# Latents' attention: four operations of the middle tiles move from VectorE to GpSimd

## The chip, the cores and the metric

The kernel runs on one core of one Trainium2 chip. The metric is the device time of one execution in microseconds (us). The engines are named as in the profile: PE (TensorE), DVE (VectorE), ACT (ScalarE), POOL (GpSimd), SP (SyncE, which only issues DMAs). Each works through its own list in the order of the program; they meet through semaphores only.

## The reference, cut to what matters

Sixteen samples of 64 latents go through a cross-attention on 1601 image tokens each, then a differential self-attention, then a mixture of 8 experts. The change lies in the self-attention.

```python
x = x + xattn(ctx_1024, layernorm(x))          # over 90% of the time
x = x + attn(layernorm(x))                     # the part that is changed
x = x + ffn(layernorm(x))                      # gates and 8 experts

# attn: 16 heads, two sub-heads of 8 each
Q, K, V = proj(Wq), proj(Wk), proj(Wv);  Q1, Q2 = split(Q);  K1, K2 = split(K)
attn = softmax(causal(Q1 K1^T / sqrt(8))) - lam * softmax(causal(Q2 K2^T / sqrt(8)))
O = attn @ V                                   # 16 heads x 16
O = O / sqrt(mean(O * O) + EPS) * rms_scale * (1 - 0.8)
return concat_heads(O) @ Wo.T
```

The 1024 latents are handled as 8 tiles of 128 rows (`TB = 8`).

## The kernel before, in words

The cross-attention fills the first 860 us. The self-attention of the 8 tiles and the experts come after it, in functions whose names begin with `tail_`: `tail_vector` is what DVE does, `tail_gpsimd` POOL, `tail_scalar` ACT, `tail_tensor` PE. Each loops over `m` from 0 to 7, and the loops are skewed against each other so that several tiles are under way. The order on each engine is written out by hand, and nothing reorders it.

What one tile t goes through, with the names used below:

- PE projects its queries and keys into PSUM (`project`), ACT copies the queries (`queries`, tile `Qs`), DVE multiplies the keys by a 0/1 mask into four spread copies (`keys`, tile `Kx`, 128x1024), and PE forms the scores in two halves (`self_scores`).
- DVE takes the maximum of each row and subtracts it, per half (`maxima`, tiles `amx` and `region`), ACT takes the exponential (`exp`), PE transposes (`transpose_exponentials`), ACT copies (`weights`), PE multiplies with the values (`weigh_values`; its semaphore is `pv`).
- DVE's `combine` divides by the sums (`arc`, `t12`), adds the two sub-heads (`Ob`), squares (`Osq`), sums (`oms`, semaphore `ms`) and scales the sum (semaphore `ms2`). POOL raises it to the power -0.5 (`inverse_rms`, semaphore `ms3`). DVE's `group_norm` multiplies (`Oc`).
- PE transposes `Oc` (`side_transposes`), ACT copies it (`side_copies`), PE multiplies by Wo (`side_products`, semaphore `side1`), DVE adds the result to x and takes the layer norm's statistics (`side_reads`, semaphore `var`), POOL takes the power for it (`ln_deviation`, semaphore `rstd`), DVE normalises (`ln_normalise`, semaphore `h2`), and PE transposes that for the experts.

Iteration m of DVE's loop is: `combine(m-1)`, `side_reads(m-1)` (which works on tile m-2), first half of `maxima(m+1)`, `keys(m+2)`, `group_norm(m-1)`, `ln_normalise(m-2)`, second half of `maxima(m+1)`. For m = 7 there are no maxima or keys, and the first part of the gates (`first0`) stands in their place. POOL's loop runs over n: `inverse_rms(n)`, then `ln_deviation(n-1)`; DVE's iteration m goes with POOL's n = m-1. For n = 3 there are two `ln_deviation`, and for n = 1 `outputs_low` follows, which belongs to the last sample of the cross-attention.

PE's iteration m is: `side_transposes(m-1)`, first half of `self_scores(m+1)`, `side_products(m-1)`, `project(m+2)`, `project_values(m+1)`, `transpose_exponentials(m, 0..1)`, second half of `self_scores(m+1)`, `transpose_exponentials(m, 2..3)`, `weigh_values(m)`. On ACT `side_copies(m-1)` stands right behind `exp` of the second half of tile m. So a side product needs the second half's maxima of the iteration before.

Of the kernel before, what the change touches and what calls it, by code (L numbers as in the profile page):

```python
# [18 lines left out]
ALU = mybir.AluOpType  # L19
# [22 lines left out]
TB = 8  # L42
SH, SD = 16, 8
# [113 lines left out]
def perceiver(nc, x, ctx_in, ln1_g, ln1_b, ln2_g, ln2_b, Wq, Wkv, Wo, aWq, aWk, aWv, aWo,  # L157
              lq1, lk1, lq2, lk2, rms_scale, gate_w, gate_b, expert_w, expert_b, out):
    es = ExitStack()
    with es:  # L160
        def sb(name, shape, dt=F32):
            return es.enter_context(nc.sbuf_tensor(name, shape, dt))
# [93 lines left out]
        pick = sb("pick", [128, 4])  # L256
# [291 lines left out]

        Qs = [sb(f"Qs{p}", [128, 2, 128]) for p in range(2)]
        Kx = [sb(f"Kx{p}", [128, 2, 4, 128]) for p in range(2)]
        VW = SD * 2 + 1
        Vb = [sb(f"Vb{p}", [128, 2, SH, 2, VW]) for p in range(2)]
# [41 lines left out]
        def side(n):  # L596
            return Turn(n - 1)
# [163 lines left out]
        def wait(eng, name, turn):  # L761
            eng.wait_ge(ta[name].sem, ta[name].upto(turn))

        def first(turn):
            return turn.off == 0
# [4 lines left out]
        def bc(ap, n):  # L770

            return ap.unsqueeze(len(ap.shape)).to_broadcast(list(ap.shape) + [n])
# [13 lines left out]
        def keys(dve, t, src):  # L786
# [4 lines left out]
            p_ = pick[:].unsqueeze(1).to_broadcast([128, 2, 4]).unsqueeze(3).to_broadcast([128, 2, 4, 128])  # L791
            nc.vector.tensor_tensor(Kx[t.off % 2][:], k_, p_, ALU.mult).then_inc(ta["kx"].sem, 1)

        def tail_vector(dve, link):
            def maxima(t, k):
                dve.wait_ge(ta["scores"].sem, ta["scores"].upto(t, k))
# [9 lines left out]
            def combine(t):  # L806
                wait(dve, "pv", t)
                pv = WW[:, :, 0:16 * VW].rearrange("p c (k d) -> p c k d", d=VW)
                nc.vector.reciprocal(arc[:], pv[:, :, :, 2 * SD]).then_inc(ta["r"].sem, 1)
                wait(dve, "r", t)  # L810
                second = arc[:].rearrange("p c (n a) -> p c n a", a=2)[:, :, :, 1]
                nc.vector.tensor_tensor(second, second, nlam[:].rearrange("p (c n) -> p c n", c=2), ALU.mult)\
                  .then_inc(ta["r2"].sem, 1)
                wait(dve, "r2", t)
                nc.vector.tensor_tensor(t12[:], pv[:, :, :, 0:2 * SD], bc(arc[:], 2 * SD), ALU.mult)\
                  .then_inc(ta["t12"].sem, 1)
                wait(dve, "t12", t)
                if not first(t):
                    wait(dve, "oc", t.plus(-1))
                v = t12[:].rearrange("p c (n a) d -> p (c n) a d", a=2)  # L820
                nc.vector.tensor_tensor(Ob[:].rearrange("p (h d) -> p h d", h=SH), v[:, :, 0, :], v[:, :, 1, :],
                                        ALU.add).then_inc(ta["ob"].sem, 1)
                wait(dve, "ob", t)
                nc.vector.tensor_tensor(Osq[:], Ob[:], Ob[:], ALU.mult).then_inc(ta["sq"].sem, 1)
                wait(dve, "sq", t)
                nc.vector.tensor_reduce(oms[:, 0, :], Osq[:].rearrange("p (h d) -> p h d", h=SH), AX.X, ALU.add)\
                  .then_inc(ta["ms"].sem, 1)
                wait(dve, "ms", t)
                nc.vector.tensor_scalar(oms[:, 1, :], oms[:, 0, :], 1.0 / (2 * SD), EPS, ALU.mult, ALU.add)\
                  .then_inc(ta["ms2"].sem, 1)  # L830

            def group_norm(t):
                wait(dve, "ms3", t)
                if not first(t):
                    wait(dve, "side0", side(t.off))
                nc.vector.tensor_tensor(Oc[:].rearrange("p (h d) -> p h d", h=SH),
                                        Ob[:].rearrange("p (h d) -> p h d", h=SH), bc(oms[:, 2, :], 2 * SD),
                                        ALU.mult).then_inc(ta["oc"].sem, 1)

            def side_reads(n):  # L840

# [67 lines left out]
            for m in range(TB):  # L909
                t = Turn(m)  # L910
                if m > 0:
                    combine(t.plus(-1))
                if m > 1:
                    side_reads(m - 1)
                if m + 1 < TB:
                    maxima(t.plus(1), 0)
                if m + 2 < TB:
                    keys(dve, t.plus(2), W[0][:, 256:512])
                if m == TB - 1:
                    first0, second0 = gating(0)  # L920
                    first0()
                if m > 0:
                    group_norm(t.plus(-1))
                if m > 1:
                    ln_normalise(dve, m - 2).then_inc(ta["h2"].sem, 1)
                if m - 1 == X1_SIDE:
                    ln_normalise(dve, TB).then_inc(ta["h"].sem, 1)
                if m + 1 < TB:
                    maxima(t.plus(1), 1)
                if m == 0:  # L930
                    reciprocals(dve, LAST)
# [24 lines left out]

        def tail_gpsimd(pool):
            def inverse_rms(t):
                wait(pool, "ms2", t)
                nc.gpsimd.tensor_tensor(oms[:, 2, :], oms[:, 1, :], mhalf[:], ALU.pow).then_inc(ta["ms3"].sem, 1)  # L960

            denominators(pool, nc.gpsimd, LAST)
            normalise_outputs(pool, nc.gpsimd, LAST)
            for n in range(TB):
                inverse_rms(Turn(n))
                if n > 0:
                    ln_deviation(pool, n - 1)
                if n == X1_SIDE:
                    ln_deviation(pool, TB)
                if n == 1:  # L970
                    outputs_low(pool, nc.gpsimd, LAST)
            ln_deviation(pool, TB - 1)
            n = 0
            for t in range(0, TB, 2):
                pool.wait_ge(ex_scaled.sem, t // 2 + 1)
                pr = prod[t // 2 % 2]
                for m in (4, 2, 1):
                    n += 1
                    nc.gpsimd.tensor_tensor(pr[:, 0:m, :], pr[:, 0:m, :], pr[:, m:2 * m, :], ALU.add)\
                      .then_inc(tail_pool.sem, 1)  # L980
                    pool.wait_ge(tail_pool.sem, n)
                pool.wait_ge(ex_xb.sem, t // 2 + 1)
                nc.gpsimd.tensor_tensor(xb[:, t, :], xb[:, t, :], pr[:, 0, :], ALU.add).then_inc(ex_even.sem, 1)


        def queries(act, t, src):
            wait(act, "projqk", t)
            nc.scalar.copy(Qs[t.off % 2][:].rearrange("p c n -> p (c n)"), src).then_inc(ta["q"].sem, 1)

        def values(act, t, src):  # L990
            wait(act, "projv", t)
# [10 lines left out]
        def tail_scalar(act, outputs, outputs_high, projected):  # L1002
# [50 lines left out]
            for m in range(TB):  # L1053
                t = Turn(m)
                if m > 1:
                    side_copies(m - 1)
                if m - 1 == PJ_SIDE:
                    projected(LAST)
                if m + 2 < TB:
                    queries(act, t.plus(2), W[0][:, 0:256])  # L1060
                if 0 < m < TB - 1:
                    values(act, t.plus(1), W[1])
                weights(t, 0)
                weights(t, 1)
                if m + 1 < TB:
                    exp(t.plus(1), 0)
                weights(t, 2)
                weights(t, 3)
                if m + 1 < TB:
                    exp(t.plus(1), 1)  # L1070
                if m == 1:
                    for k in range(2):
                        outputs_high(LAST, k)
# [39 lines left out]
        def tail_tensor(pe, side_item, weigh):  # L1113
# [31 lines left out]
            def weigh_values(t):  # L1145
                wait(pe, "vb", t)
                if more(t):
                    wait(pe, "vb", t.plus(1))
                if t.off + 2 < TB:
                    wait(pe, "kx", t.plus(2))  # L1150
                for r in range(4):
                    pe.wait_ge(ta["et_out"].sem, ta["et_out"].upto(t, r))
                    for h in range(4):
                        c, n = h // 2, 2 * r + h % 2
                        for j in range(2):
                            ins = mm(W[c][64 * j:64 * j + 64, 2 * VW * n:2 * VW * n + 2 * VW],
                                     ET[t.off % 2][:, r, h, 64 * j:64 * j + 64],
                                     Vb[t.off % 2][:, j, 8 * c + n].rearrange("p a d -> p (a d)"),
                                     start=True, stop=True)
                ins.then_inc(ta["pv"].sem, 1)  # L1160
# [588 lines left out]
        def _(act):  # L1749
# [125 lines left out]
            def slot(b, prep=True, post=True, stats=True):  # L1875
                old = b.plus(-1)
                for u in range(UNITS):
# [12 lines left out]
                    if b is LAST and u == H_AT:  # L1890
                        early_columns_out(act)
                    if b is LAST and u == TILE0_AT:
                        queries(act, Turn(0), W[0][:, 0:256])
                        values(act, Turn(0), W[1])
                    if b is LAST and u == KEYS1_AT:
                        queries(act, Turn(1), W[0][:, 0:256])
                    if b is LAST and u == VALUES1_AT:
                        values(act, Turn(1), W[1])

# [372 lines left out]
```

## Time and profile before

| | us |
|---|---|
| median of 3 runs (977.25 to 979.66) | 978.41 |
| the profiled execution | 982.4 |
| its span | 980.6 |
| DVE busy in 907.50 to 918.00 (one tile, m = 5) | 10.12 of 10.50 |
| POOL busy in the same stretch | 3.42 of 10.50 |

The profile is that of one execution, and its span starts with the first instruction. PE, PEld (weight loads), DVE, ACT and POOL have their own rows; a row's start plus its duration is its end, and the next instruction of an engine can start a little before that. "idle before" names what ended the engine's wait. PEclk 1.00 is TensorE at 2.4 GHz, 0.50 at 1.2 GHz. In this span DVE's loop iterations m = 2 to 7 begin, with the reciprocal of L809, at 869.50, 883.21, 896.22, 907.58, 917.88 and 927.03, and the last `combine` at 935.30.

### The profile page before, as it was taken

The page shows a single profiled execution, that of the slowest core. Times are in us where ns is not written, and L with a number is a line of the kernel's source. Part 1 is how long each engine was busy: PE and PEld are TensorE (multiplying, and loading weights), DVE is VectorE, ACT ScalarE, POOL GpSimd, SP SyncE. Part 2 cuts the span into 40 slices and gives each one's busy share as a digit, 9 for nine tenths or more (in the row PEclk, how much of TensorE's full clock was granted, in tenths as well). Part 3 has the DMA queues.
Part 4 walks back from the last instruction along what each step waited for, and adds up shares of the span by engine and source line. Part 5 has one row for each costly group of instructions (what it writes and reads, how often), then busy time and mean ns, then how long its engine had stood idle before and what let it go on. Part 6 is the DMA issues. An engine that isn't in the chain of part 4 may idle for free.

```text
span 980.6 us, 20490 instructions
## 1 busy us (share of the span) xinstructions
PE 925.7 (94%) x8246; PEld 497.7 (51%) x8246; DVE 795.9 (81%) x1591; ACT 701.2 (72%) x1003; POOL 377.5 (38%) x376
## 2 busy tenths in 40 slices
PE   8679999999999999999999999999999998979985
PEld 5444445454545454545454545454545454557642
DVE  5969798989798989898979797979897845768945
ACT  4576778786878787878787787878787667545531
POOL 6562134433443435343434333434342304163342
PEclk9799999999999999999999999999999999979977
DMA  6212030302120303030212121121212000000000
GB/s 207 70 21 61 6 86 11 82 12 81 12 80 13 81 12 81 12 81 18 74 22 72 30 63 37 56 35 59 42 39 37 22 2 22 23 3 23 2 6 16
DMA packets 74565, 41.95 MB, mean 43 GB/s; under 512 B 62276, under 2 KB 69864, under 8 KB 74472
## 3 DMA queue, kind: packets, MB, share of 16 engines
q1 hardware_dynamic: 74184, 39.60, 16.2%
q8 instruction: 65, 1.06, 0.4%
q10 hardware_dynamic: 288, 1.05, 0.3%
q14 instruction: 28, 0.23, 0.1%
HBM read 25.98 MB, written 0.59 MB: 27 GB/s over the span
## 4 chain that ended last, share of the span: by engine, by line
PE 79%; DVE 12%; ACT 4%; issue 2%; POOL 1%; DMA 1%; POOLq 0%; ACTq 0%; DVEq 0%
PE S L2122 9%; PE S L2113 9%; PE OA L2146 9%; PE S L2116 8%; PE OA L2152 8%; PE OA L2149 8%; PE WW L2058 8%; PE WW L2085 1%; PE WW L2086 1%; PE WW L2087 1%; PE WW L2045 1%; PE S L1205 1%; DVE region L1517 1%; PE WW L2047 1%; PE WW L2046 1%
## 5 line engine op out<-in xcount | busy, mean ns | idle before, releaser
L1833 ACT ACTIVATE region<-S,sigma 128x1024 f16<-128x1024 f32 x208 | 231.6, 1113 | 142.2 <-PE S L2122 142.2
L1517 DVE TENSOR_TENSOR region<-S,region 128x1024 f16<-128x1024 f32 x208 | 252.4, 1214 | 47.7 <-ACT S L1837 47.6
L1505 DVE TENSOR_REDUCE mx<-WW 128x1 f32<-128x512 f32 (+1 forms) x480 | 262.6, 583 | 29.6 <-PE WW L2058 22.4
L1837 ACT ACTIVATE S<-S,sigma 128x1024 f32<-128x1024 f32 x208 | 224.3, 1078 | 0.0
L1652 POOL TENSOR_TENSOR xk<-raw,xk 128x508 f16<-128x508 f32 x64 | 63.3, 998 | 170.6 <-DVE xk L1384 170.6
L2058 PE MATMUL WW<-xT,region 128*128 128x512 f16 x360 | 124.8, 381 | 4.1 <-DVE region L1496 2.1
L2113 PE MATMUL S<-region,xT 128*128 128x512 f16 (+1 forms) x416 | 124.7, 381 | 3.4 <-DVE region L1517 1.7
L2122 PE MATMUL S<-region,xT 128*128 128x512 f16 (+1 forms) x416 | 124.2, 380 | 0.0
L2116 PE MATMUL S<-region,xT 128*128 128x512 f16 (+1 forms) x416 | 124.2, 380 | 0.0
L2146 PE MATMUL OA<-region,xk 128*128 128x512 f16 (+1 forms) x416 | 123.9, 379 | 0.0
L2149 PE MATMUL OA<-region,xk 128*128 128x512 f16 (+1 forms) x416 | 123.7, 379 | 0.0
L2152 PE MATMUL OA<-region,xk 128*128 128x512 f16 (+1 forms) x416 | 123.7, 379 | 0.0
L538 POOL TENSOR_TENSOR region<-region,rb 128x512 f32<-128x512 f32 x32 | 40.6, 1270 | 128.8 <-DMA rb<-inv_dram 128.8
L546 POOL TENSOR_TENSOR ew<-region,o_hi 128x1024 f16<-128x1024 f32 x32 | 68.0, 2126 | 57.1 <-ACT o_hi L1814 57.1
L1771 ACT ACTIVATE raw<-raw,smc 128x128 f32<-128x128 f32 (+1 forms) x187 | 86.1, 486 | 0.0
L2122 PEld LDWEIGHTS S<-region,xT 128*128 128x128 f16 (+1 forms) x416 | 41.2, 99 | 48.9 <-issue 0.5
L2116 PEld LDWEIGHTS S<-region,xT 128*128 128x128 f16 (+1 forms) x416 | 41.1, 99 | 49.0 <-issue 0.5
L2149 PEld LDWEIGHTS OA<-region,xk 128*128 128x128 f16 (+1 forms) x416 | 40.6, 98 | 49.1
L2152 PEld LDWEIGHTS OA<-region,xk 128*128 128x128 f16 (+1 forms) x416 | 40.6, 98 | 49.1
L2058 PEld LDWEIGHTS WW<-xT,region 128*128 128x128 f16 x360 | 34.9, 97 | 55.7 <-DVE region L1496 14.0
L1641 POOL TENSOR_TENSOR smc<-smc,mhalf 128x13 f32<-128x13 f32 x16 | 38.9, 2433 | 60.5 <-DVE smc L456 60.5
L2113 PEld LDWEIGHTS S<-region,xT 128*128 128x128 f16 (+1 forms) x416 | 34.2, 99 | 44.0 <-issue 17.4
(315 smaller groups left out, 1851.0 us busy)
## 6 DMA issues: line engine op xcount, KB each, us to landing
raw<-ctx SPq DMA_DIRECT2D x16, 768.0 KB
rb<-inv_dram SPq DMA_DIRECT2D x16, 512.0 KB, 3.5
xT<-xk SPq DMA_TRANSPOSE x48, 3.2
left_row<-left_pT SPq DMA_DIRECT2D x48, 2.0 KB
raw<-ctx SPq DMA_DIRECT2D x16, 32.5 KB
WO_lo<-L_xattn_Wq ACTq DMA_DIRECT2D x1, 512.0 KB, 3.8
WO_hi<-L_xattn_Wkv ACTq DMA_DIRECT2D x1, 512.0 KB, 4.7
lx<-x SPq DMA_DIRECT2D x1, 512.0 KB, 6.3
```

The lines of the kernel that those rows point to most:

```text
L1505: nc.vector.tensor_reduce(mx[:, r, c:c + 1], W[BANK[("m", n)]][:, 0:width], AX.X, ALU.max)\
L1517: nc.vector.tensor_tensor(p_lo[k], src, p_hi[k], ALU.subtract).then_inc(lo_done.sem, 1)
L1771: ins = nc.scalar.activation(x_[0:r, t, :], x_[0:r, t, :], ACT.Identity, bias=smc[0:r, 2, t:t + 1], scale=smc[0:r, 1, t:t + 1])
L1833: nc.scalar.activation(p_hi[k], src, ACT.Exp, scale=sigma[:, 0:1])
L1837: nc.scalar.activation(src, src, ACT.Exp, scale=sigma[:, 0:1]).then_inc(e_done.sem, 1)
L2058: ins = mm(w, rows, xT_hi[p][:, 512 * c:512 * c + 512], start=True, stop=True)
L2113: mm(banks[r, k, :], hi, q_hi[p][:, cols(qc, k)], start=True, stop=False)
L2116: mm(banks[r, k, :], hi, q_lo[p][:, cols(qc, k)], start=False, stop=False)
L2122: ins = mm(banks[r, k, :], lo, q_hi[p][:, cols(qc, k)], start=False, stop=True)
L2146: mm(dst[k], hi, ph[r, cols[k]], start=first, stop=False)
L2149: mm(dst[k], hi, pl[r, cols[k]], start=False, stop=False)
L2152: ins = mm(dst[k], lo, ph[r, cols[k]], start=False, stop=last)
```

## The change

For the tiles `2 <= t < 7` (`norm_shared`) the sum of the sub-heads, the squares and the multiplication into `Oc` are issued by POOL; the sum over the squares and its scaling stay on DVE, but are issued after the first half of the maxima (`mean_squares`). For the tiles `t >= 4` (`keys_shared`) ACT copies keys together with queries, 512 columns in place of 256, into a new tile `QK`, and POOL spreads the keys from there. PE's `weigh_values` waits for ACT's copy instead of the spread keys.

```diff
-        Qs = [sb(f"Qs{p}", [128, 2, 128]) for p in range(2)]
+        QK = [sb(f"QK{p}", [128, 2, 2, 128]) for p in range(2)]
+        Qs = [QK[p][:, 0] for p in range(2)]
...
+        def norm_shared(t):
+            return 2 <= t.off < TB - 1
+
+        def keys_shared(t):
+            return t.off >= 4
+
+        def squares(eng, vec, t):
+            if not first(t):
+                wait(eng, "oc", t.plus(-1))
+            v = t12[:].rearrange("p c (n a) d -> p (c n) a d", a=2)
+            vec.tensor_tensor(Ob[:].rearrange("p (h d) -> p h d", h=SH), v[:, :, 0, :], v[:, :, 1, :],
+                              ALU.add).then_inc(ta["ob"].sem, 1)
+            wait(eng, "ob", t)
+            vec.tensor_tensor(Osq[:], Ob[:], Ob[:], ALU.mult).then_inc(ta["sq"].sem, 1)
+
+        def scaled(eng, vec, t):
+            if not first(t):
+                wait(eng, "side0", side(t.off))
+            vec.tensor_tensor(Oc[:].rearrange("p (h d) -> p h d", h=SH), Ob[:].rearrange("p (h d) -> p h d", h=SH),
+                              bc(oms[:, 2, :], 2 * SD), ALU.mult).then_inc(ta["oc"].sem, 1)
...
+                if not first(t) and norm_shared(t.plus(-1)):
+                    wait(dve, "ob", t.plus(-1))
                 nc.vector.tensor_tensor(t12[:], pv[:, :, :, 0:2 * SD], bc(arc[:], 2 * SD), ALU.mult)\
                   .then_inc(ta["t12"].sem, 1)
...
+                if not norm_shared(t):
+                    wait(dve, "t12", t)
+                    squares(dve, nc.vector, t)
+                    mean_squares(t)
+
+            def mean_squares(t):
                 wait(dve, "sq", t)
...
                 if m + 1 < TB:
                     maxima(t.plus(1), 0)
-                if m + 2 < TB:
+                if m > 0 and norm_shared(t.plus(-1)):
+                    mean_squares(t.plus(-1))
+                if m + 2 < TB and not keys_shared(t.plus(2)):
                     keys(dve, t.plus(2), W[0][:, 256:512])
...
-                if m > 0:
+                if m > 0 and not norm_shared(t.plus(-1)):
                     group_norm(t.plus(-1))
...
             def inverse_rms(t):
+                if norm_shared(t):
+                    wait(pool, "t12", t)
+                    squares(pool, nc.gpsimd, t)
                 wait(pool, "ms2", t)
                 nc.gpsimd.tensor_tensor(oms[:, 2, :], oms[:, 1, :], mhalf[:], ALU.pow).then_inc(ta["ms3"].sem, 1)
+                if norm_shared(t):
+                    wait(pool, "ms3", t)
+                    scaled(pool, nc.gpsimd, t)
+
+            def shared_keys(t):
+                wait(pool, "q", t)
+                pool.wait_ge(ta["scores"].sem, ta["scores"].upto(t.plus(-2), 1))
...
+                nc.gpsimd.tensor_tensor(Kx[t.off % 2][:], k_, p_, ALU.mult).then_inc(ta["kx"].sem, 1)
...
+                if 4 <= n + 3 < TB:
+                    shared_keys(Turn(n + 3))
                 if n == 1:
                     outputs_low(pool, nc.gpsimd, LAST)
...
+            n = 2 if keys_shared(t) else 1
+            if keys_shared(t) and t.off >= 6:
+                wait(act, "kx", t.plus(-2))
+            nc.scalar.copy(QK[t.off % 2][:, 0:n].rearrange("p a c n -> p (a c n)"), src[:, 0:256 * n]).then_inc(ta["q"].sem, 1)
...
-                    wait(pe, "kx", t.plus(2))
+                    wait(pe, "q" if keys_shared(t.plus(2)) else "kx", t.plus(2))
```

On DVE, in iteration m = 5 of the kernel before, this stands between the two halves of the maxima of tile 6 (`amx` and `region` are the maxima and the differences, `Kx` the keys of tile 7, `Oc` of tile 4, `raw` with `ln` the layer norm of tile 3):

```order
L798 TENSOR_REDUCE amx<-S 128x16 [waits ta_scores]
L802 TENSOR_TENSOR region<-S,amx 128x1024 [waits ta_et,ta_max]
L792 TENSOR_TENSOR Kx<-WW,pick 128x1024 [waits ta_scores,ta_q]
L836 TENSOR_TENSOR Oc<-Ob,oms 128x256 [waits ta_side0,ta_ms3]
L680 TENSOR_SCALAR raw<-raw,ln 128x128 [waits ta_rstd]
L798 TENSOR_REDUCE amx<-S 128x16 [waits ta_scores]
```

The same place of the changed kernel:

```order
L820 TENSOR_REDUCE amx<-S 128x16 [waits ta_scores]
L824 TENSOR_TENSOR region<-S,amx 128x1024 [waits ta_et,ta_max]
L848 TENSOR_REDUCE oms<-Osq 128x16 [waits ta_sq]
L851 TENSOR_SCALAR oms<-oms 128x16 [waits ta_ms]
L681 TENSOR_SCALAR raw<-raw,ln 128x128 [waits ta_rstd]
L820 TENSOR_REDUCE amx<-S 128x16 [waits ta_scores]
```

The two operations on `oms`, whose second one signals `ms2`, stood ahead of the first maxima and now stand right ahead of the one that waits for `rstd`.

On POOL, from n = 0 to n = 2 of the kernel before (the powers for `oms` and for the layer norm `ln`, and `outputs_low`, which writes `ew`):

```order
L960 TENSOR_TENSOR oms<-oms,mhalf 128x16 [waits ta_ms2] x2
L675 TENSOR_TENSOR ln<-ln,mhalf 128x1 [waits ta_var]
L546 TENSOR_TENSOR ew<-region,o_hi 128x2x512 [waits o_hi_done] x2
L960 TENSOR_TENSOR oms<-oms,mhalf 128x16 [waits ta_ms2]
L675 TENSOR_TENSOR ln<-ln,mhalf 128x1 [waits ta_var]
```

The same of the changed kernel, up to the keys of tile 5:

```order
L983 TENSOR_TENSOR oms<-oms,mhalf 128x16 [waits ta_ms2] x2
L676 TENSOR_TENSOR ln<-ln,mhalf 128x1 [waits ta_var]
L993 TENSOR_TENSOR Kx<-QK,pick 128x1024 [waits ta_scores,ta_q]
L546 TENSOR_TENSOR ew<-region,o_hi 128x2x512 [waits o_hi_done] x2
L805 TENSOR_TENSOR Ob<-t 128x256 [waits ta_oc,ta_t12]
L808 TENSOR_TENSOR Osq<-Ob 128x256 [waits ta_ob]
L983 TENSOR_TENSOR oms<-oms,mhalf 128x16 [waits ta_ms2]
L813 TENSOR_TENSOR Oc<-Ob,oms 128x256 [waits ta_side0,ta_ms3]
L676 TENSOR_TENSOR ln<-ln,mhalf 128x1 [waits ta_var]
L993 TENSOR_TENSOR Kx<-QK,pick 128x1024 [waits ta_scores,ta_q]
```

The power that signals `rstd` (L675, now L676) stands behind the wait for `ms2` in both. Between them there is now `Oc` too, behind it the keys, and the keys of tile 4 stand ahead of `outputs_low`. The last six rows repeat for n = 3 (with two L676) and n = 4; for n = 5 and 6 the keys fall away.

## Rows read from the trace of the kernel before

**Rows 1.** Windows: busy us of PE, PEld, DVE, ACT, POOL, then PEclk, DMA

```profile
907.50:918.00 10.50, 9.88 (x141) 7.30 (x140) 10.12 (x21) 6.22 (x13) 3.42 (x2) 1.00 0.01 2
...
929.00:931.00 2.00, 2.00 (x11) 2.00 (x11) 1.59 (x7) 0.00 (x0) 1.02 (x1) 0.50 0.00 0
```

**Rows 2.** Timeline of DVE, m = 5: start, us, instruction, count, [idle before <-releaser]

```profile
907.58 0.35 DVE L809 RECIPROCAL arc<-WW 128x32 f32<-128x32 f32 x1
...
908.90 0.42 DVE L821 TENSOR_TENSOR Ob<-t 128x256 f32<-128x256 f32 x1
...
909.82 0.42 DVE L826 TENSOR_REDUCE oms<-Osq 128x16 f32<-128x256 f32 x1
910.28 0.17 DVE L829 TENSOR_SCALAR oms<-oms 128x16 f32<-128x16 f32 x1
910.36 0.28 DVE L845 TENSOR_TENSOR raw<-OA,raw 128x128 f32<-128x128 f32 x1
...
911.37 1.22 DVE L798 TENSOR_REDUCE amx<-S 128x16 f32<-128x1024 f32 x1
...
913.76 1.22 DVE L792 TENSOR_TENSOR Kx<-WW,pick 128x1024 f32<-128x1024 f32 x1
914.89 0.41 DVE L836 TENSOR_TENSOR Oc<-Ob,oms 128x256 f32<-128x256 f32 x1
915.23 0.34 DVE L680 TENSOR_SCALAR raw<-raw,ln 128x128 f32<-128x128 f32 x1
915.48 1.22 DVE L798 TENSOR_REDUCE amx<-S 128x16 f32<-128x1024 f32 x1
...
917.88 0.35 DVE L809 RECIPROCAL arc<-WW 128x32 f32<-128x32 f32 x1
```

**Rows 3.** Timeline of PE and ACT around the side product, m = 5 and m = 7

```profile
909.40 0.71 PE L1185 MATMUL OA<-woaT,OcT 128*128 128x128 f32 x4 [0.61 <-ACT xk L1024]
909.95 0.29 PE L1189 MATMUL OA<-gwT,xk 128*128 128x8 f32 x2
...
915.68 2.06 PE L1156 MATMUL WW<-Vb,region 128*64 128x34 f32 x64
...
928.68 1.22 PE L1185 MATMUL OA<-woaT,OcT 128*128 128x128 f32 x4 [1.27 <-ACT xk L1024]
```

**Rows 4.** Timeline of DVE: waits for `side1` in m = 3 and m = 7, later starts

```profile
888.70 0.29 DVE L845 TENSOR_TENSOR raw<-OA,raw 128x128 f32<-128x128 f32 x1 [2.61 <-PE OA L1189]
...
925.89 1.23 DVE L802 TENSOR_TENSOR region<-S,amx 128x1024 f32<-128x1024 f32 x1
...
930.17 0.29 DVE L845 TENSOR_TENSOR raw<-OA,raw 128x128 f32<-128x128 f32 x1 [0.28 <-PE OA L1189]
...
935.30 0.36 DVE L809 RECIPROCAL arc<-WW 128x32 f32<-128x32 f32 x1 [1.52 <-PE WW L1156]
```

**Rows 5.** POOL: timeline, m = 5 (two rows), then groups by line and form

```profile
910.53 2.91 POOL L960 TENSOR_TENSOR oms<-oms,mhalf 128x16 f32<-128x16 f32 x1 [7.43 <-DVE oms L829]
913.41 0.54 POOL L675 TENSOR_TENSOR ln<-ln,mhalf 128x1 f32<-128x1 f32 x1
...
L979 POOL TENSOR_TENSOR region<-region 128x256 f32<-128x256 f32 x4 | 2.9, 733 | 0.3
...
L519 POOL TENSOR_TENSOR srow<-region 1x1024 f32<-1x1024 f32 x16 | 37.5, 2341 | 25.3 <-ACT region L532 14.0 <-ACT region L1848 10.2
```

**Rows 6.** Timeline of DVE and POOL at the same times, at 816 and at 876

```profile
816.12 2.76 DVE L657 TENSOR_SCALAR raw<-raw,sm 128x128 f32<-128x128 f32 x3
...
816.31 1.27 POOL L538 TENSOR_TENSOR region<-region,rb 128x512 f32<-128x512 f32 x1 [2.39 <-DMA rb<-inv_dram]
817.55 1.26 POOL L539 TENSOR_TENSOR region<-region,rb 128x512 f32<-128x512 f32 x1
...
875.84 4.21 POOL L546 TENSOR_TENSOR ew<-region,o_hi 128x1024 f16<-128x1024 f32 x2
...
878.61 1.73 DVE L836 TENSOR_TENSOR Oc<-Ob,oms 128x256 f32<-128x256 f32 x1
```

More of the change, by code:

```diff
@@ L814, in combine @@
                 wait(dve, "r2", t)
+                if not first(t) and norm_shared(t.plus(-1)):
+                    wait(dve, "ob", t.plus(-1))
                 nc.vector.tensor_tensor(t12[:], pv[:, :, :, 0:2 * SD], bc(arc[:], 2 * SD), ALU.mult)\
                   .then_inc(ta["t12"].sem, 1)
[L817 to L824, printed above, removed]
+                if not norm_shared(t):
[3 more added lines that the diff above has]
+            def mean_squares(t):
                 wait(dve, "sq", t)
@@ L833, in group_norm @@
                 wait(dve, "ms3", t)
[L834 to L838, printed above, removed]
+                scaled(dve, nc.vector, t)
             def side_reads(n):
@@ L958, in inverse_rms @@
             def inverse_rms(t):
+                if norm_shared(t):
+                    wait(pool, "t12", t)
+                    squares(pool, nc.gpsimd, t)
                 wait(pool, "ms2", t)
                 nc.gpsimd.tensor_tensor(oms[:, 2, :], oms[:, 1, :], mhalf[:], ALU.pow).then_inc(ta["ms3"].sem, 1)
+                if norm_shared(t):
[4 more added lines that the diff above has]
+                pool.wait_ge(ta["scores"].sem, ta["scores"].upto(t.plus(-2), 1))
+                k_ = QK[t.off % 2][:, 1].unsqueeze(2).to_broadcast([128, 2, 4, 128])
+                p_ = pick[:].unsqueeze(1).to_broadcast([128, 2, 4]).unsqueeze(3).to_broadcast([128, 2, 4, 128])
+                nc.gpsimd.tensor_tensor(Kx[t.off % 2][:], k_, p_, ALU.mult).then_inc(ta["kx"].sem, 1)
             denominators(pool, nc.gpsimd, LAST)
@@ L987, in queries @@
             wait(act, "projqk", t)
-            nc.scalar.copy(Qs[t.off % 2][:].rearrange("p c n -> p (c n)"), src).then_inc(ta["q"].sem, 1)
+            n = 2 if keys_shared(t) else 1
+            if keys_shared(t) and t.off >= 6:
+                wait(act, "kx", t.plus(-2))
+            nc.scalar.copy(QK[t.off % 2][:, 0:n].rearrange("p a c n -> p (a c n)"), src[:, 0:256 * n]).then_inc(ta["q"].sem, 1)
         def values(act, t, src):
@@ L1059, in tail_scalar @@
                 if m + 2 < TB:
-                    queries(act, t.plus(2), W[0][:, 0:256])
+                    queries(act, t.plus(2), W[0])
                 if 0 < m < TB - 1:
@@ L1892, in slot @@
                     if b is LAST and u == TILE0_AT:
-                        queries(act, Turn(0), W[0][:, 0:256])
+                        queries(act, Turn(0), W[0])
                         values(act, Turn(0), W[1])
                     if b is LAST and u == KEYS1_AT:
-                        queries(act, Turn(1), W[0][:, 0:256])
+                        queries(act, Turn(1), W[0])
                     if b is LAST and u == VALUES1_AT:
```

## The prediction

> **What bounds the kernel now.** The change touches the eight tiles of the self-attention alone, so I read the windows first. In the stretch of one tile DVE is busy 10.12 of 10.50 us and POOL 3.42 [rows 1]: at first sight DVE is the engine to relieve. PE is busy 9.88 in the same stretch, so it must be asked whether PE follows close behind. The timeline of DVE answers what one iteration is made of [rows 2]: it begins at 907.58 and the next one at 917.88, 10.30 us, with no idle time between. Adding the sub-heads and squaring take 908.90 to 909.82, 0.92 us; the side reads 910.36 to 911.37, 1.01; each half of the maxima 2.39 or 2.40 (911.37 to 913.76, 915.48 to 917.88); the keys 1.13; Oc 0.34; the layer norm's L680 0.25. What moves away is therefore 1.13 + 0.34 + 0.92 = 2.39 us of a tile with keys.
>
> PE and ACT set a second limit. I call S the moment at which DVE ends the second half of the maxima; it lies 0.08 behind the next start. S of m = 4 is at 907.66. From it the exponential and two or three copies on ACT lead to the side product at 909.40 and to its last product at 909.95 + 0.29 = 910.24, and the rest of PE's list ends with the values at 915.68 + 2.06 = 917.74 [rows 3]. That is 2.6 us to `side1` and 10.1 to `pv`. DVE's next reader of `side1` is L845 at 910.36, 2.70 behind S [rows 2]: the 0.92 us in front of it only just covered that wait.
>
> **What the change puts in place of the work.** No work is added; it is the order on two engines that matters. On DVE `ms2` is now signalled behind the first half of the maxima, and the very next instruction is L680, which waits for `rstd`. On POOL the power that signals `rstd` stands behind the one that waits for `ms2`. Before, `ms2` came 3 us ahead and the power ran beside the side reads, the maxima and the keys: 910.53 to 913.41, and the layer norm's power 0.54 behind it, done at 913.95, 1.3 us before L680 needed it [rows 2, 5]. Now nothing stands between on DVE, and the whole of POOL's chain becomes a stall of DVE. Behind L680 on DVE wait the second half of the maxima, so S, and with it ACT's next exponential, the side product and the next iteration.
>
> The serial piece, from the first half of the maxima to L680:
> - sum and scaling on DVE, 909.82 to 910.28 + 0.17: 0.63 [rows 2]
> - to POOL, 910.45 to 910.53: 0.08; the power to the next start: 2.88 [rows 5]
> - Oc on POOL, 128x256: 0.73, by L979 of that size; the trace has no broadcast operand there [rows 5]. By L546, 2.1 for 1024 columns, it would be 0.53 [rows 6]
> - the layer norm's power: 0.54 [rows 5]; release of DVE about 0.06, like the 0.08 above.
>
> That is 4.92. L680 ought to start then, but POOL goes straight on to the keys, whose two waits have long been met, and it needs no semaphore's way for that. What that does to L680 shows at 816: L657 is the same operation with the same shapes. Three of them take 2.76 us where 0.25 each is the pace, while POOL's L538 and L539 start at 816.31 and 817.55. The second one is held until 817.6 and the third until 818.8, each to the end of one POOL instruction, and POOL is not slowed [rows 6]. Oc at 878.61 likewise lasts 1.73 in place of 0.41, to 0.3 us past the end of L546 at 880.05 [rows 2, 6]. So I let L680 be held by the keys: 128x1024 of f32 takes 2.34 as L519, on one partition, but in the same number of columns [rows 5]; the bounds are 2.1 (L546) and 2.5 (two L538) [rows 6]. Held, the piece is 4.92 + 2.34 = 7.26; not held, 4.92. Both ends are kept.
>
> The Trainium skill says of this (SBUF — State Buffer, "Who interferes with whom") that VectorE and GpSimd share a port pair as an exclusive lock, so that the second to issue is blocked until the first ends, and that tensor_scalar takes part in it only in a 2-port mode. The trace agrees on the blocking, with 1.3 us for a held L657. By that rule, too, the hold hangs on who issues first: POOL first gives the 7.26, DVE first the 4.92, a rival below.
>
> **The sum, tile by tile.** Against the old 1.13 + 0.34 of keys and Oc in the same place:
> - m = 3 (tile 2's norm, tile 5's keys): 7.26 - 1.47 = +5.79. Its side reads begin at 888.70 because PE is busy with the last sample's projection [rows 4], so earlier gains and losses vanish there, the freed 0.92 too. But that projection needs `outputs_low`, now behind tile 4's keys: ACT's copy, two thirds of a microsecond at most, then 2.34 of keys push its 4.21 us from 875.84 [rows 6] to about 883.1 or, with DVE's Oc and L680 let in between, 883.7. PE asked for it at about 883.5: +0.3, from 0 to 1.
> - m = 4: a second layer-norm power, 0.54 more: +6.33.
> - m = 5: +5.79.
> - m = 6: no keys, neither before nor now: 4.92 - 0.34 = +4.58.
> - m = 4, 5 and 6: DVE now reaches L845 at about 1.3 behind the start and waits for `side1`. At PE's full clock that comes about 0.1 earlier than L845's old start. But PE, with some 6 us of each iteration idle, will hardly keep that clock: after an idle time of 1.27 the side product took 1.22 in place of 0.71 (rows of 909.40 and 928.68), at 0.50 [rows 1, 3], and L845 started at 930.17, 3.05 behind S at 927.12 [rows 4], +0.35 on the 2.70. Three times: +1.05; the lower end is -0.3.
> - m = 7: 3.05 to the side reads, 1.02 for them, 4.92, 0.26 for L680: 9.25 from S to the last `combine`, where before `pv` came at 8.18 (935.30 less 927.12) [rows 4]. +1.07. The gates' first part is hidden by the power.
> - behind it: PE waits about 1.1 us for the last L680 before it transposes for the experts, and the gap of 1.27 before 928.68 lowered the clock [rows 1, 3]. The four expert products and the side product behind them could take up to 2.4 longer. I take half, +1.2.
>
> ACT's wider copy hides in ACT's idle time (busy 6.22 of 10.50 [rows 1]), PE's earlier release from `kx` in the stall, and Ob and Osq on POOL, 1.5 us, in the wait for `side1` and the maxima. If the last cover failed, it would cost what sticks out, at most 1.5 a tile; 1.01 + 2.39 + 1.3 lie over it.
>
> Sum: 5.79 + 0.3 + 6.33 + 5.79 + 4.58 + 1.05 + 1.07 + 1.2 = 26.1. The profiled execution took 982.4 with a span of 980.6, so the changed one would take 1008.5 with a span near 1006.7. The median of the runs shown is 978.41, 4.0 below; the stretch has no transfer that could differ with it, so I add the same amount: 1004.5. In the terms of a tile: an iteration of 10.3 becomes one of about 16.4.
>
> **Rivals.**
> - DVE gets through ahead of the keys, or is not held by them. For it: DVE's release and POOL's next instruction are a tenth of a microsecond apart. Against it: at 816 POOL's second instruction started in time while DVE was waiting. Three times 2.34 less: 19.1, so 997.5. With PE's full clock as well 995.
> - PE becomes the bound. If its clock stayed at 0.50 through an iteration, the 8.3 us from 909.40 to 917.74 would be 16.7 and S to `pv` 18.4, more than the new 16.4 for m = 5 and 14 for m = 6, and m = 7 some 5 longer: 11 us more, 1015. Against it: at 929 to 931 the clock was 0.50 with PE fully busy, and the values of that iteration were done 8.2 us behind S all the same.
> - Not slower: DVE really is relieved. That would need POOL's piece to be hidden, so that an iteration is 2.6 to `side1`, 1.01, 2.39, 0.63, 0.25 and 2.40, 9.3 us, against PE's 10.1 from S to `pv`, which begins up to a microsecond earlier: 0.6 to 0.9 a tile gained in m = 3, 4 and 5, nothing in m = 6, 2.5 in all, 976. It decides as soon as `ms2` reaches POOL 4.9 us before L680 is due. The order on the two engines speaks against it: L680 is next behind `ms2`.
> - POOL is quicker than its rows or I have missed a cover, and the loss is about half: 990.
>
> **How the numbers follow.** The forecast has 0.62, with a range of its own of 1000 to 1008; no hold 0.20; PE as the bound 0.06; half the loss 0.06; not slower 0.06. 994 to 1010 leaves out the last three, 0.18. A difference of 0.3%, 2.9 us, is what a measurement here can tell from none: faster by more 0.03, within it 0.03, slower 0.94.
>
> **What would show it.** DVE idle for about 4 us ahead of L681 (the old L680) in m = 3 to 6, released by POOL; Oc on POOL near 0.73 and the keys near 2.34; L681 itself lasting over 2 us in m = 3, 4 and 5 and 0.34 in m = 6; DVE idle a good microsecond ahead of the side reads; PEclk under 1.00 in most iterations. I am wrong if L681 follows `ms2` without a wait, or if iterations stay near 10 us.

## The result, and the profile after

The changed kernel took 1003.59 us (median of 4 runs, 1001.55 to 1005.97) against 978.71: a ratio of 1.0256, 95% interval 1.023 to 1.0283, or 24.9 us. 1004.5 was forecast. Run again on another chip it was 1005.44 against 980.66, ratio 1.0241 (1.0202 to 1.0279). The profiled execution took 1005.97 with a span of 1004.2.

Each kernel has one profile of one execution: the one before took 982.4, which is 3.7 over its median, the changed one 2.4 over. So the small rows of the table, at the start and at the end, say less than the large ones. The starts of DVE's iterations (reciprocal of L809, now L831) in the two profiles show where the time went:

| | before | after | difference | predicted |
|---|---|---|---|---|
| up to m = 2 | 869.50 | 872.07 | +2.57 | 0 |
| m = 2 | 13.71 | 13.93 | +0.22 | 0 |
| m = 3 | 13.01 | 17.95 | +4.94 | +6.09 |
| m = 4 | 11.36 | 17.41 | +6.05 | +6.68 |
| m = 5 | 10.30 | 15.77 | +5.47 | +6.14 |
| m = 6 | 9.15 | 14.04 | +4.89 | +4.93 |
| m = 7 | 8.27 | 9.36 | +1.09 | +1.07 |
| from the last `combine` on | 45.30 | 43.67 | -1.63 | +1.2 |
| span | 980.6 | 1004.2 | +23.6 | +26.1 |

This is DVE in m = 5 of the changed kernel (timeline: start, duration, instruction, count, idle time before and what ended it), to be laid beside [rows 2]:

```profile
921.36 0.35 DVE L831 RECIPROCAL arc<-WW 128x32 f32<-128x32 f32 x1
...
924.67 0.29 DVE L863 TENSOR_TENSOR raw<-OA,raw 128x128 f32<-128x128 f32 x1 [2.02 <-PE OA L1227]
...
925.68 1.22 DVE L820 TENSOR_REDUCE amx<-S 128x16 f32<-128x1024 f32 x1
926.93 1.23 DVE L824 TENSOR_TENSOR region<-S,amx 128x1024 f32<-128x1024 f32 x1
928.07 0.41 DVE L848 TENSOR_REDUCE oms<-Osq 128x16 f32<-128x256 f32 x1
928.52 0.17 DVE L851 TENSOR_SCALAR oms<-oms 128x16 f32<-128x16 f32 x1
932.92 1.90 DVE L681 TENSOR_SCALAR raw<-raw,ln 128x128 f32<-128x128 f32 x1 [4.23 <-POOL ln L676]
934.74 1.21 DVE L820 TENSOR_REDUCE amx<-S 128x16 f32<-128x1024 f32 x1
```

DVE has two idle times where it had none: 2.02 us for `side1` and 4.23 us for POOL. Behind the second one L681, the layer norm, takes 1.90 us instead of the 0.34 of L680. The same place on POOL, beside [rows 5]:

```profile
928.77 2.92 POOL L983 TENSOR_TENSOR oms<-oms,mhalf 128x16 f32<-128x16 f32 x1 [4.62 <-DVE oms L851]
931.76 0.62 POOL L813 TENSOR_TENSOR Oc<-Ob,oms 128x256 f32<-128x256 f32 x1
932.35 0.54 POOL L676 TENSOR_TENSOR ln<-ln,mhalf 128x1 f32<-128x1 f32 x1
932.85 1.89 POOL L993 TENSOR_TENSOR Kx<-QK,pick 128x1024 f32<-128x1024 f32 x1
938.49 0.73 POOL L805 TENSOR_TENSOR Ob<-t 128x256 f32<-128x256 f32 x1 [3.75 <-DVE t L839]
939.30 0.61 POOL L808 TENSOR_TENSOR Osq<-Ob 128x256 f32<-128x256 f32 x1
```

The first four, in a row, fill the time from `ms2` to L681's end: the keys start 0.07 before L681 and end at 934.74, and DVE's next instruction starts then. PE in the same iteration, beside [rows 3] (timeline), and below it the granted clock (windows: busy us of PE, PEld, DVE, ACT and POOL, then PEclk, DMA):

```profile
923.18 1.22 PE L1223 MATMUL OA<-woaT,OcT 128*128 128x128 f32 x4 [2.29 <-ACT xk L1062]
924.20 0.43 PE L1227 MATMUL OA<-gwT,xk 128*128 128x8 f32 x2
```

```profile
918.00:920.00 2.00, 1.14 (x8) 0.60 (x12) 2.00 (x3) 0.00 (x0) 0.71 (x1) 1.00 0.00 0
920.00:922.00 2.00, 0.89 (x16) 0.31 (x9) 1.90 (x5) 0.52 (x1) 0.00 (x0) 0.90 0.00 0
922.00:924.00 2.00, 0.82 (x4) 0.82 (x5) 0.65 (x1) 1.13 (x4) 1.20 (x2) 0.50 0.00 0
...
921.36:937.13 15.77, 12.90 (x141) 9.14 (x141) 9.24 (x16) 6.42 (x12) 7.23 (x6) 0.78 0.01 1
```

PE idles 2.29 us ahead of the side product and runs it at 1.2 GHz, in 1.22 us where m = 5 had needed 0.71.

### The profile page after: what moved, and what is told of

It is laid out like the page before. It is cut to its first block, busy times and chain, and to the rows that moved or that the text cites. A ratio compares the mean times of both kernels' runs of the same rounds, so it can differ in the third digit from the quotient of the medians.

```text
span 1004.2 us, 20498 instructions
## 1 busy us (share of the span) xinstructions
PE 934.9 (93%) x8246; PEld 503.0 (50%) x8246; DVE 792.0 (79%) x1572; ACT 702.0 (70%) x1003; POOL 395.0 (39%) x395
## 3 DMA queue, kind: packets, MB, share of 16 engines
q10 hardware_dynamic: 288, 1.05, 0.3%
## 4 chain that ended last, share of the span: by engine, by line
PE 76%; DVE 10%; issue 5%; POOL 4%; ACT 4%; DMA 1%; POOLq 0%; ACTq 0%; DVEq 0%
PE S L2160 9%; PE S L2151 9%; PE OA L2184 8%; PE S L2154 8%; PE OA L2187 8%; PE OA L2190 8%; PE WW L2096 8%; POOL oms L983 2%; PE WW L2123 1%; PE WW L2124 1%; PE WW L2125 1%; PE WW L2083 1%; DVE region L1555 1%; PE WW L2085 1%; PE WW L2084 1%
## 5 line engine op out<-in xcount | busy, mean ns | idle before, releaser
L1543 DVE TENSOR_REDUCE mx<-WW 128x1 f32<-128x512 f32 (+1 forms) x480 | 262.3, 582 | 29.7 <-PE WW L2096 22.4
L538 POOL TENSOR_TENSOR region<-region,rb 128x512 f32<-128x512 f32 x32 | 40.6, 1270 | 129.7 <-DMA rb<-inv_dram 129.7
L546 POOL TENSOR_TENSOR ew<-region,o_hi 128x1024 f16<-128x1024 f32 x32 | 68.3, 2134 | 58.8 <-ACT o_hi L1852 58.8
```

Source lines behind the costliest of these rows:

```text
L1543: nc.vector.tensor_reduce(mx[:, r, c:c + 1], W[BANK[("m", n)]][:, 0:width], AX.X, ALU.max)\
```

## The experiments

The theory: the time is lost where DVE waits, ahead of the layer norm, for POOL's chain started by a late `ms2`, and in the hold of that layer norm by the keys. The rivals: POOL's load or the data path that it shares with DVE costs by itself; or the keys on POOL do; or the forecast hold is something else. All comparisons are with the kernel before on the same chip, unless another is named. In the diffs `...` marks what is left out.

**Norms alone.** The keys go back to DVE.

```diff
         def keys_shared(t):
-            return t.off >= 4
+            return False
...
-                if 4 <= n + 3 < TB:
+                if False:
```

> Keys back on DVE and ACT's copy back to 256 columns; the norms of tiles 2 to 6 stay on POOL. My theory (the loss is DVE's wait at the layer norm for the serial chain sum, power, Oc, layer-norm power, plus the hold by the keys): the keys, 1.13 us, stand inside that wait and there is no hold, so m = 3 and 5 lose 4.85 - 1.13 - 0.34 = 3.4 each against the kernel before, m = 4 3.9, m = 6 4.5, the late side product 1 in all, m = 7 1.1: about 17, so 996 (993 to 998); L681 lasts 0.34 and DVE waits about 3.1 us ahead of it. Rival A (the keys on POOL are what costs): within 3 us of the kernel before. Rival B (the keys do not matter): as the changed kernel, 1003.6.

Measured: 999.4 (994.98 to 1003.46), ratio 1.0177 (1.0117 to 1.0237). The median is 3.4 above what was expected and 1.4 outside the range, with an interval of 12 us. The profile is plainer. DVE waits 3.10 us in m = 5, and L681 lasts 0.35:

```profile
926.07 0.17 DVE L851 TENSOR_SCALAR oms<-oms 128x16 f32<-128x16 f32 x1
926.15 1.22 DVE L793 TENSOR_TENSOR Kx<-WW,pick 128x1024 f32<-128x1024 f32 x1
930.48 0.35 DVE L681 TENSOR_SCALAR raw<-raw,ln 128x128 f32<-128x128 f32 x1 [3.10 <-POOL ln L676]
```

Its iterations m = 3 to 7 are longer than before by 3.39, 4.33, 3.92, 4.29 and 1.08, 17.0 in all, which is the forecast 17; the rest lies mainly ahead of m = 2, which its profile reaches 3.6 us later. Rival A falls: the norms alone cost most of it. Rival B, that the keys do not matter, is not settled by the median, whose interval overlaps that of the change; in the profiles the same five iterations lose 17.0 here and 22.4 with the keys on POOL.

**Keys alone.** The norms go back to DVE.

```diff
         def norm_shared(t):
-            return 2 <= t.off < TB - 1
+            return False
```

> Only the keys of tiles 4 to 7 on POOL, the norms all on DVE. My theory: the power now again runs early, so DVE hardly waits; what the keys free on DVE (1.13) is taken back where Oc or the layer norm, due at about the same time, is held for the rest of POOL's 1.89 us of keys: 976 to 980, no difference from the kernel before (978.7) that can be told; one of Oc and L681 lasts over 1 us in m = 4 and 5. Rival A (keys on POOL cost by themselves): 983 or more. Rival B (no hold, the work just leaves DVE): 975.5.

Measured: 980.76 (10 runs) against 978.81, ratio 1.001 (0.9987 to 1.0034): no difference that can be told, and no gain, though the median lies 0.8 above the expected range. Rival A (983 or more) falls, and so does rival B, since the hold is there. DVE and POOL at the same times in m = 4 and m = 5 (one fence for each engine):

```profile
904.23 2.03 DVE L813 TENSOR_TENSOR Oc<-Ob,oms 128x256 f32<-128x256 f32 x1
906.18 0.59 DVE L681 TENSOR_SCALAR raw<-raw,ln 128x128 f32<-128x128 f32 x2
...
915.25 0.41 DVE L813 TENSOR_TENSOR Oc<-Ob,oms 128x256 f32<-128x256 f32 x1
915.59 1.92 DVE L681 TENSOR_SCALAR raw<-raw,ln 128x128 f32<-128x128 f32 x1
```

```profile
904.09 1.89 POOL L993 TENSOR_TENSOR Kx<-QK,pick 128x1024 f32<-128x1024 f32 x1
...
915.41 2.01 POOL L993 TENSOR_TENSOR Kx<-QK,pick 128x1024 f32<-128x1024 f32 x1
```

In m = 4 the keys are first by 0.14, and Oc, with two inputs in SBUF, is held to 0.28 past their end. In m = 5 Oc is first by 0.16: the keys take 0.12 longer, and the hold falls on L681. Each time it is about 1.6 us, more than the 1.13 that left DVE. The iterations did not all come out alike: m = 4 and 5 took 0.50 and 1.47 more than before, m = 3 took 0.27 less, and m = 7 1.05 less, with its side product at full clock (0.71 instead of 1.22). That the total is the same is in part such a balance.

**Keys in two instructions.**

```diff
-                k_ = QK[t.off % 2][:, 1].unsqueeze(2).to_broadcast([128, 2, 4, 128])
-                p_ = pick[:].unsqueeze(1).to_broadcast([128, 2, 4]).unsqueeze(3).to_broadcast([128, 2, 4, 128])
-                nc.gpsimd.tensor_tensor(Kx[t.off % 2][:], k_, p_, ALU.mult).then_inc(ta["kx"].sem, 1)
+                p_ = pick[:].unsqueeze(2).to_broadcast([128, 4, 128])
+                for c in range(2):
+                    k_ = QK[t.off % 2][:, 1, c].unsqueeze(1).to_broadcast([128, 4, 128])
+                    ins = nc.gpsimd.tensor_tensor(Kx[t.off % 2][:, c], k_, p_, ALU.mult)
+                ins.then_inc(ta["kx"].sem, 1)
```

> The whole change, but POOL spreads the keys in two instructions of 512 columns in place of one of 1024. If L681 is held to the end of one POOL instruction, it lasts about 1.0 us in place of 1.9 in m = 3, 4 and 5: three times 0.9 less, about 1001. Rival (L681 is slow beside POOL for its whole work, or for another reason): it stays at 1.9 and the time at 1003.6.

Measured: 1001.03 (997.08 to 1003.57), ratio 1.0205 (1.0153 to 1.0257); next to the change's 1.0256 and 1.0241 that is in the expected direction, but the intervals overlap. L681 in m = 5 decides it: 1.05 where it had been 1.90 (DVE, then POOL).

```profile
928.00 1.05 DVE L681 TENSOR_SCALAR raw<-raw,ln 128x128 f32<-128x128 f32 x1 [4.23 <-POOL ln L676]
928.97 1.21 DVE L820 TENSOR_REDUCE amx<-S 128x16 f32<-128x1024 f32 x1
```

```profile
927.92 2.04 POOL L994 TENSOR_TENSOR Kx<-QK,pick 128x512 f32<-128x512 f32 x2
```

The hold ends with one POOL instruction, not with POOL's work: that is an exclusive hold. Iterations m = 3 and 5 are 0.69 and 0.85 shorter than the change's. The expected 0.9 did not come in m = 4 (17.30 against 17.41): it has two L681, which took 2.06 together, so each was held by a half. The Trainium skill's rule (SBUF — State Buffer, "Who interferes with whom"), that the second to issue is blocked until the first ends, agrees with this: 1.05 and 1.90 follow the length of the POOL instruction.

**The sum of squares early.**

```diff
+                if m > 0 and norm_shared(t.plus(-1)):
+                    mean_squares(t.plus(-1))
                 if m + 1 < TB:
                     maxima(t.plus(1), 0)
-                if m > 0 and norm_shared(t.plus(-1)):
-                    mean_squares(t.plus(-1))
```

> The whole change, but DVE issues the sum of squares and its scaling ahead of the first half of the maxima. My theory: POOL's chain of 4.2 us then runs beside 2.39 us of maxima, and DVE's wait ahead of L681 shrinks by those 2.39 in m = 3 to 6 (to about 1.9), the hold by the keys stays: 4 x 2.4 = 9.6 less than the changed kernel, 994 (991 to 996). Rival (POOL's load is what costs): no difference from 1003.

Measured: 995.52 (991.6 to 996.47), ratio 1.014 (1.0105 to 1.0176). Against the change itself on that chip, 1005.44, it is 9.9 less; 9.6 was expected. DVE's waits ahead of L681 in m = 3 to 6 are 1.85, 2.38, 1.84 and 1.85 instead of 4.23, 4.76, 4.23 and 4.23: 2.4 less each, the first half of the maxima. In m = 5:

```profile
924.98 1.90 DVE L681 TENSOR_SCALAR raw<-raw,ln 128x128 f32<-128x128 f32 x1 [1.84 <-POOL ln L676]
```

The iterations m = 3 to 6 are 2.38, 3.10, 2.79 and 2.99 shorter than the change's; from m = 4 on, the side product took 0.71 or 0.81 instead of 1.22 as well. The POOL instructions are the same in kind and number, so its load is not the cause.

**The layer norm's power first.** On POOL, the powers that signal `rstd` go ahead of the wait for `ms2`. `deviations(n)` holds the two calls of `ln_deviation` that are taken out below.

```diff
                     squares(pool, nc.gpsimd, t)
+                    deviations(t.off)
                 wait(pool, "ms2", t)
...
-                if n > 0:
-                    ln_deviation(pool, n - 1)
-                if n == X1_SIDE:
-                    ln_deviation(pool, TB)
+                if not norm_shared(Turn(n)):
+                    deviations(n)
```

> The whole change, but on POOL the layer norm's power stands right behind the squares, ahead of the wait for ms2. My theory: DVE's wait of 4.2 us ahead of L681 goes; what is late next is the keys of the next tile but one, behind the power and Oc, which PE needs ahead of the side product, so an iteration is 10 to 11.5 us and the time 980 to 987, about 983; L681 lasts 0.34. Rival (the loss is POOL's load or its port traffic and not this order): 998 or more.

Measured: 989.58 (986.68 to 993.3), ratio 1.0101 (1.0071 to 1.013), 6.6 above the expected 983 and 2.6 outside its range. The rival (998 or more) falls. The wait ahead of L681 is gone and L681 lasts 0.34; 14 of the 25 us are gone with this order. What came late next is what was named, PE's wait for the keys, and its size was missed. PE at the start of m = 6:

```profile
925.67 0.44 PE L1210 MATMUL OA<-ident,Oc 128*128 128x128 f32 x2 [0.33 <-POOL Oc L813]
925.94 0.27 PE L1213 MATMUL OA<-ident,raw 128*128 128x128 f32 x1
927.56 1.01 PE L1167 MATMUL S<-mask,identb 128*128 128x512 bf16 x2 [1.35 <-issue]
928.51 1.98 PE L1173 MATMUL S<-Kx,QK 32*64 32x256 f32 x16
930.42 1.22 PE L1228 MATMUL OA<-woaT,OcT 128*128 128x128 f32 x4
```

POOL's keys ended at 925.57 + 1.89 = 927.46, and PE starts the scores 0.1 later. The 1.35 us is called "issue", since the profile found no releaser for it; in the program PE waits there for `kx`, the signal of the keys. After it PE ran at 1.2 GHz, and scores and side product took nearly twice as long: the side reads began at 931.91 after 3.69 us of waiting. Iterations alternate: m = 4 and 6 with this fall of the clock took 15.16 and 14.11 us. In m = 5 PE waited 1.24 us for the keys, the clock stayed at 1.00, and the iteration took 11.99. What decides between the two is not shown.

**Both orders mended.** The two edits above together.

> Sum of squares ahead of the first maxima on DVE, and the layer norm's power ahead of the wait for ms2 on POOL. My theory: DVE waits for POOL nowhere, the keys are ready about when the values end, so an iteration is PE's and ACT's 10 us: near the kernel before, 978 (974 to 982); L681 lasts 0.34. Rival (two engines' traffic and late keys go on costing): 985 or more, as in the run with the layer norm's power first.

Measured: 982.44 (10 runs) against 980.66, ratio 1.0025 (1.0007 to 1.0043). That is 0.4 outside the expected range and still slower than before, by 1.8 us. But with the whole of the work on POOL as in the change, 23 of the 25 us are gone, and the rival (985 or more) falls. Iterations m = 3 to 6 are 12.51, 10.44, 10.86 and 9.52, close to the 13.01, 11.36, 10.30 and 9.15 of before, and PEclk is 1.00 in each of them; DVE idles over 1.3 us in m = 4 to 6 waiting for `side1`. In m = 5:

```profile
909.35 0.29 DVE L863 TENSOR_TENSOR raw<-OA,raw 128x128 f32<-128x128 f32 x1 [1.76 <-PE OA L1232]
...
913.29 0.34 DVE L681 TENSOR_SCALAR raw<-raw,ln 128x128 f32<-128x128 f32 x1
```

So DVE is relieved, and it waits for PE's and ACT's path instead. Where the last 1.8 us lie the profiles do not tell: those of the kernel before and of this one take the same time to m = 2, and m = 3 to 7 are 2.0 us shorter here.

**Keys alone, norms behind the maxima.** As in the run with the keys alone, but to avoid the hold, Oc and the layer norm are issued behind the second half of the maxima, whose scores are read from PSUM.

```diff
         def norm_shared(t):
-            return 2 <= t.off < TB - 1
+            return False
...
+                late = 3 <= m < TB - 1
+                if late:
+                    maxima(t.plus(1), 1)
...
-                if m + 1 < TB:
+                if m + 1 < TB and not late:
                     maxima(t.plus(1), 1)
```

> Norms on DVE, keys of tiles 4 to 7 on POOL, and for m = 3 to 6 DVE issues Oc and the layer norm behind the second maxima instead of ahead of it. If the hold by the keys is what took back the 1.13 us a tile of the run with the keys alone, neither Oc nor L681 lasts over 0.6 now and the time is 975.5 (973 to 978). Rival (PE's and ACT's path of 10.1 us sets the end, so DVE's relief is worth nothing): 978 to 981, as with the keys alone.

Measured: 979.61 (10 runs) against 980.66, ratio 0.9981 (0.9964 to 0.9998), the one version whose median is below that of the kernel before, by 1.05 us. In m = 5:

```profile
914.81 1.23 DVE L820 TENSOR_REDUCE amx<-S 128x16 f32<-128x1024 f32 x1 [0.99 <-PE S L1171]
...
917.21 0.41 DVE L813 TENSOR_TENSOR Oc<-Ob,oms 128x256 f32<-128x256 f32 x1
917.54 0.34 DVE L681 TENSOR_SCALAR raw<-raw,ln 128x128 f32<-128x128 f32 x1
```

The hold is gone in m = 3 to 5 (Oc 0.41 or 0.42, one L681 0.34), but 975.5 was not reached, and the median is 1.6 above the expected range: DVE now waits for the second half of the scores, 1.03, 0.22 and 0.99 us. The rival was right about the size: PE's path leaves little to gain. That the hold is what took back the 1.13 of the run with the keys alone, these rows show; the medians of the two runs are too near each other to show it.

**The change again.** The changed kernel unaltered.

> The changed kernel unaltered, on this chip, to compare the others with: 1003.6 (1001 to 1006), for any theory.

Measured: 1005.44 (1000.93 to 1006.68), ratio 1.0241. Its iterations are within 0.05 us of those in the table for m = 3 to 7.

## Why the prediction was right

The three things that carry the forecast came as named: DVE's wait for POOL's chain, the hold behind it, and the late side product. Two small terms of the sum did not come, and one was worked out too long. That the total is so near is partly luck, as shown at the end of this section.

**The order, not the work.** The step "the whole of POOL's chain becomes a stall of DVE" held: 928.07 to 932.92 is 4.85, predicted 4.92, and the runs with the sum early and with the layer norm's power first show it by taking parts of it away. Oc took 0.62 instead of 0.73. L681 waited for POOL in every one of these iterations, so the rival in which DVE is relieved falls.

**The hold.** It came in m = 3, 4 and 5 as forecast, POOL ahead of DVE each time by 0.06 or 0.07, but it was dearer in the sum than on the chip: what follows L681 was late by 1.90 - 0.08 - 0.25 = 1.57 instead of 2.34. Of these 0.77 us, 0.45 are the keys, which took 1.89, below the lower bound of 2.1 taken from L546. Another 0.25 are a slip of the sum: a held L681 ends with the keys, so its own 0.25 lies inside the 7.26, but only the 1.47 of keys and Oc were taken off, not the 0.25 of L680. The last 0.07 is POOL's lead. Three times 0.77 is 2.3, the largest error among the terms of the iterations. The nearest row was not near: L519 has as many columns, but reads two different full rows, while the keys read 256 values and a mask over and over. The run with the keys in two parts shows that the hold is what was thought, and that DVE gets through ahead of the keys, the first rival, did not happen.

**The side product.** Predicted +0.35 in m = 4 to 6; measured from S it is 3.27, 3.23 and 3.05 against 2.70, so +0.57, +0.53 and +0.35. The side product ran at 1.2 GHz there, as supposed. The 6 us of idle PE that this was argued from were not there: in m = 5 PE was busy 12.90 of 15.77, since part of its work ran at the lower clock. The rival in which the clock stays at 0.50 through an iteration did not come either; PEclk over m = 5 is 0.78.

**The tail of POOL's old work.** The +0.3 for a late `outputs_low` in m = 3 did not come. It was pushed back by the keys of tile 4, but was done at 880.92 + 4.42 = 885.34, and PE read its result 0.95 us later, straight behind the product that does not need it:

```profile
880.92 4.42 POOL L546 TENSOR_TENSOR ew<-region,o_hi 128x1024 f16<-128x1024 f32 x2
```

```profile
886.26 0.19 PE L2123 MATMUL OA<-o_hi,WO_hi 128*128 128x64 f16 x1
886.29 0.19 PE L2124 MATMUL OA<-ew,WO_hi 128*128 128x64 f16 x1
```

DVE's side reads of m = 3 began 5.49 us behind the iteration's start in both profiles. The +0.22 in m = 2 is not this term: that iteration took 13.13 to 14.07 in the nine profiles other than the one of before, whatever stood on POOL.

**The end.** m = 7 came out at +1.09 for +1.07. Behind it I took +1.2 for a fall of the clock at the experts' first products; they took 1.89, as before (1.88), and the step fails. The end was 1.63 shorter instead, mainly since more of the experts' later products ran at full clock: of two sets of four that took 3.78 and 3.48, the second now took 1.98. That is not shown to be the change's doing. In the ten profiles of this study the second set ran at full clock, and the end took 43.5 to 43.8 us, in five (the change twice, keys alone, keys alone with norms behind the maxima, layer norm's power first); in the other five the end took 45.3 to 46.6. Both kinds hold versions that are slow and versions that are not.

**What stays open.** The profile of the change reaches m = 2 2.57 us later than the one of before, though its program is the same up to there except for the queries' tile. PE was at 0.50 to 0.75 from 819 to 827, where the profile of before was back at 1.00 at 823. The ten profiles of this study reach m = 2 between 868.75 and 873.07, and the six whose program is that of the change up to there (the change twice, layer norm's power first, keys in halves, sum early, both orders) between 868.75 and 872.40. Of these six, the two in which PEclk stayed at 1.00 from 819 to 827, keys in halves and both orders, were the first, at 868.75 and 869.48. So I count the 2.6 us as scatter that goes with the clock there; why the clock fell in some executions and not in others is open, and a small part may still be the change's. The hit on the total is in part such compensation: the iterations were forecast 2.3 too long and the end 2.8 too long, and the start gave 2.6 back. Of the 24.9 us between the medians, m = 2 to 7 account for 22.7; the other 2 cannot be placed with one profile of the kernel before.

## What to carry to other kernels

When work goes to an idle engine, look at what the receiving engine has next in its list and who waits for that: here one signal issued 2.4 us later on DVE and one power issued behind it on POOL turned 2.4 us of relief a tile into about 5 us of loss, and both were to be seen in two order listings. Here a layer norm, or a multiplication with two SBUF inputs, on VectorE next to one GpSimd instruction over 512 or 1024 columns waited for the end of that instruction; the maxima, which read their scores from PSUM, ran beside such work in their usual 1.2 us (keys alone, norms behind the maxima). And before relieving the busiest engine, work out the next path (here 10.1 us against 10.3): with both orders mended the whole change was still 1.8 us slower than before, and the best version, with the keys alone, gained 1.05.

## What the runs showed of the hardware

- GpSimd's tensor_tensor depends on its operands. At 512 columns of f32 the keys, with both inputs repeated, took 1.04 us, L538 with two full inputs 1.27; at 1024 columns the keys took 1.89, L519 with two full inputs, though on one partition, 2.34. At 256 columns two different inputs took 0.73, the same tile twice (Osq) 0.61, one input broadcast (Oc) 0.62.
- Not every GpSimd instruction holds VectorE. In m = 7 of the changed kernel operations on `lg` with two SBUF inputs ran in 0.20 to 0.22 us inside the power of 2.92, as in the kernel before. The power is long, but of 128x16; that its small size is the reason is not shown.

```profile
956.08 0.22 DVE L887 TENSOR_TENSOR lg<-lg,g 128x40 f32<-128x40 f32 x1
956.34 0.20 DVE L888 TENSOR_TENSOR lg<-lg,rank 128x40 f32<-128x40 f32 x1
```

```profile
956.02 2.92 POOL L983 TENSOR_TENSOR oms<-oms,mhalf 128x16 f32<-128x16 f32 x1 [2.07 <-DVE oms L851]
```

- A stall of one engine can cost twice where it lets PE idle: in m = 5 to 7 of the changed kernel PE waited 2.1 to 3.6 us ahead of the side product, which took 1.22 instead of 0.71. The last gap alone doesn't decide it: with the row sum early, waits of 2.12 and 2.29 us were followed by 0.71 and 0.81, and in m = 4 of the changed kernel 1.22 followed a wait of 0.66.
